# Sigmoid masks of a graph's first tile moved ahead of the last sums, the second tile's spread between evictions, one lookup ahead of the sums, and a normalization ahead of a bit count

## The reference

```python
vals = jnp.where(nd[..., None], x[:, None, :, :], jnp.inf)
s = jnp.sort(vals, axis=2)                  # per node, over its kept neighbours, per channel
nv = nd.sum(2)
for tau, w in zip((0.25, 0.5, 0.75), (0.25, 0.5, 0.25)):
    pos = tau * jnp.maximum(nv - 1, 0)      # lo = floor, hi = ceil, frac
    agg = agg + w * (v_lo + frac * (v_hi - v_lo))
h = jax.nn.relu((x + agg) @ W1 + b1); y = (h @ W2 + b2) * mask
```

## Time and profile before

| | |
|---|---|
| median of 3 runs | 3866.15 us (3860.3 to 3867.21) |
| the profiled execution | 3872.41 us, of which the span is 3870.6 us |
| VectorE busy | 3180.9 us, 82% |
| TensorE matmul busy | 2635.5 us, 68% |
| ScalarE busy | 1949.1 us, 50% |
| one graph in the steady part | 187.7 us |

### The profile page before, as it was taken

One profiled execution on the slowest core, in us unless ns is written; L12 is line 12 of the kernel. 1 busy time (PEld: TensorE's weight loads), 2 busy tenths in 40 slices (PEclk: granted clock), 3 DMA queues, 4 the chain that ended last, 5 costly groups with the idle time before them and its releaser, 6 DMA issues. The chain is left out here.

```text
span 3870.6 us, 48616 instructions
## 1 busy us (share of the span) xinstructions
PE 2635.5 (68%) x16944; PEld 1215.1 (31%) x17098; DVE 3180.9 (82%) x5858; ACT 1949.1 (50%) x2672; POOL 8.0 (0%) x21
## 2 busy tenths in 40 slices
PE   0000155777777877778777778787878787887897
PEld 0000022333333333333333333333323333333665
DVE  8999988888888888787878787878888887855676
ACT  2114444565656565656565646565656565553232
POOL 0000000000000000000000000000000000000000
PEclk6555576898889888888898989888989898887777
DMA  1001001323232323222232323232322222332111
GB/s 36 0 14 46 0 11 22 57 40 56 35 57 37 55 38 56 37 54 39 52 42 50 50 41 57 33 59 35 56 43 48 45 49 44 40 56 39 44 33 33
DMA packets 242849, 158.50 MB, mean 41 GB/s; under 512 B 126504, under 2 KB 228026, under 8 KB 242362
## 3 DMA queue, kind: packets, MB, share of 16 engines
q1 hardware_dynamic: 238490, 154.49, 23.8%
q10 hardware_dynamic: 4128, 1.05, 0.2%
HBM read 40.14 MB, written 14.70 MB: 14 GB/s over the span
## 5 line engine op out<-in xcount | busy, mean ns | idle before, releaser
L1002 ACT ACTIVATE hot<-bcast,consts 128x1024 bf16<-128x1024 f32 x744 | 829.8, 1115 | 487.4 <-PE bcast L567 486.8
L1386 DVE SCALAR_TENSOR_TENSOR prod<-near,consts,rows 128x512 f32<-128x512 bf16 x768 | 566.5, 746 | 323.1 <-PE rows L580 219.5
L580 PE MATMUL rows<-hot,table 128*64 128x512 bf16 x4608 | 729.6, 428 | 115.0 <-DVE prod L1386 103.8
L554 PE MATMUL ring<-member,neigh_t 128*128 128x512 bf16 x1924 | 516.3, 407 | 179.4 <-ACT words L963 149.1
L589 PE MATMUL found_bank<-prod,consts 128*64 128x512 f32 x1536 | 446.3, 656 | 3.9 <-DVE prod L1386 3.9
L567 PE MATMUL bcast<-idx_t,consts 32*128 32x512 f16 x1488 | 315.4, 421 | 171.6 <-ACT hot L1002 158.3
L580 PEld LDWEIGHTS rows<-hot,table 128*64 128x64 bf16 x4608 | 225.9, 116 | 408.8 <-issue 320.4
L554 PEld LDWEIGHTS ring<-member,neigh_t 128*128 128x128 bf16 x2048 | 182.6, 103 | 527.7 <-ACT words L963 193.6
L492 PE MATMUL ring<-identb,adj_b 128*128 128x128 bf16 x256 | 35.6, 272 | 380.1 <-ACT adj_b L890 367.5
L567 PEld LDWEIGHTS bcast<-idx_t,consts 32*128 32x128 f16 x1488 | 71.0, 92 | 540.3 <-ACT hot L1002 364.6
L963 ACT ACTIVATE words<-ring 128x512 uint16<-128x512 f32 x256 | 146.5, 592 | 146.8 <-PE ring L554 146.0
(11 more groups left out here) (332 smaller groups left out, 4371.5 us busy)
## 6 DMA issues: line engine op xcount, KB each, us to landing
near<-idx_bt SPq DMA_DIRECT2D x768, 128.0 KB
late<-in_adj_dram SPq DMA_DIRECT2D x16, 1024.0 KB, 5.6
adjt_d<-late SPq DMA_DIRECT2D x16, 512.0 KB, 2.8
adj_l<-adjt_d SPq DMA_DIRECT2D x16, 512.0 KB, 5.6
adj_s<-adjt_d SPq DMA_DIRECT2D x16, 512.0 KB, 3.5
parts_d<-parts SPq DMA_DIRECT2D x6, 512.0 KB, 5.1
table<-parts_d SPq DMA_DIRECT2D x192, 16.0 KB, 2.2
out_dram<-x_all SPq DMA_DIRECT2D x4, 512.0 KB, 3.8
```

The costliest lines, as they stand in the source:

```text
L554: ins = mm(ring[u % 2][:, :], kept_t[:, j, P * i:P * i + P], member[:, j, n // 2, 512 * (n % 2):512 * (n % 2) + 512], start=(j == 0), stop ...
L580: ins = mm(rows[u % 2][C * h:C * h + C, :], table[:, s, GROUPS * h + g8, :], hot[:, u % HOT, h, :], start=(s == 0), stop=(s == 2))
L1002: run(hot[:, u % HOT].rearrange(flat), spread_bank(l, u)[0][:, 0:2, :].rearrange(flat), ACT.Relu, bias=eq_bias[:, :]).then_inc(S["hot_read ...
L1386: stt(out=prod[:, u % DEEP, :], in0=near[:, u % NEAR, :], scalar=iota_b[:, :], in1=rows[u % 2][:, :], op0=ALU.is_equal, op1=ALU.mult).then ...
```

## The change

Four moves, with nothing added or removed. The three masks of tile 0 go from `select` to the end of the preceding `region`, behind the copies of tile 0's chunks and ahead of `keep_sum` and tile 1's first chunks. Tile 1's three masks go between the copies of its own chunks and the hots, and each hot of `select` stands one place further ahead. TensorE's `units(l, 3)` (spread 4 and lookup 2) goes ahead of chunk 5 and the two sums. VectorE's `pop` (eight instructions) goes behind `gcn_start` and behind unit 30.

```diff
 # TensorE, select
                 chunk(b, 1, 4)
+                units(l, 3)
                 chunk(b, 1, 5)
                 sum_first(b, 0)
                 sum_size(b, 0)
-                units(l, 3)
                 chunk(b, 1, 6)
 # ScalarE, select
                 units(l, 3)
-                for i in range(2):
-                    for k in range(TAUS):
-                        mask(b, i, k)
                 chunk(b, 1, 2)
                 chunk(b, 1, 3)
+                mask(b, 1, 0)
+                units(l, 4)
                 chunk(b, 1, 4)
-                units(l, 4)
+                units(l, 5)
                 chunk(b, 1, 5)
+                mask(b, 1, 1)
                 keep_sums(b, 0)
                 chunk(b, 1, 6)
-                units(l, 5)
+                units(l, 6)
                 chunk(b, 1, 7)
-                units(l, 6)
+                mask(b, 1, 2)
 # ScalarE, region (and the same two lines ahead of the first graph)
                         chunk(p, 0, n)
                         if n == 1:
                             tag(p, 0)
+                    for k in range(TAUS):
+                        mask(p, 0, k)
                 if l is not None:
                     keep_sum(l, d)
 # VectorE, region
                 if p is not None:
                     clear_own(p)
-                if t_of is not None:
-                    pop(wl, x2, x4, x8, t)
                 units(l, STEP[5])
                 if d is not None:
                     gcn_start(d)
+                if t_of is not None:
+                    pop(wl, x2, x4, x8, t)
                 if p is not None:
                     members(p, 1)
```

More of the change, by code:

```diff
@@ L1129, in _ @@
                     tag(0, 0)
+            for k in range(TAUS):
+                mask(0, 0, k)
             for b in range(B):
```

## The result

| | median (range) of 4 runs each | profiled span | clock over the span |
|---|---|---|---|
| before | 3866.68 us (3860.3 to 3867.34) | 3870.6 us | 0.811 |
| after | 3796.47 us (3793.05 to 3804.74) | 3797.5 us | 0.815 |

The ratio is 0.9825 [0.9805, 0.9845]: 70 us faster. I had forecast 107 us and 3759, with a range that ends at 3812. So about a third of the gain is missing.

A forecast was written before the change was run, and what follows sets the result against it. VectorE was taken to bound the kernel, idle 31.6 us per 187.7 us graph, mostly waiting for tile 0's masks. 15 x 5.2 + 14 x 1.9 + 2 = 107 us off 3866 gave 3759, range 3735 to 3812.

The forecast's parts named there:

- Tile 0 (15 x 5.2 + 2 = 80): First tile of a graph: masks made ahead gain 5.2 us in 15 graphs, plus 2 us in the first graph.
- a chunk at the low clock: Tile 1's chunks 2 and 3 ahead of the transposes: one at the low clock makes the delay 3.3 us, not 2.5.
- a steady 1.5: Line 1434 (now 1438), tile 0's size multiply: its 9.15 us wait becomes 1.5, ended by TensorE's transposes.
- my middle: Value 3 of tile 0: 5.2 us gain per graph, taken between 6.2 (all high clock) and 4.3 (low up to lookup 2).
- The 2 us of the first graphs: First graph, with no units beside its tile 0: a smaller wait of the same kind, taken as 2 us.
- the 7.6 of the wait: Shortening of the wait at tile 0's size multiply, forecast to go from 9.15 us to 1.5.
- The `pop` move (14 x 1.9 = 27): In `region`: `x1_ready` 3.6 us earlier lets value 32 follow value 31, gaining 1.9 us in 14 graphs.
- My lower bound: For the `pop` move: 1.2 us per graph, if the low clock holds up lookup 33.
- nothing later eats the lead: Behind tile 0: the lead of about 5 us passes to the next tiles, whose waits keep their size.
- The rival of 0.22: Tile 0: TensorE's clock stays low or `near` loads are late; gain only 30 to 80 us; chance 0.22.
- The slower case: Low clock holds on into tile 1, behind the sums, to 1798: about 94 us slower, 3960; chance 0.05.
- the masks of tile 1: Third mask ends near 1785.4, line 1434 asks at 1789: cover 3.6 us; VectorE waiting for them would refute the forecast.

The follow-up runs named there:

- a1_no_pop: The kernel after with `pop` back ahead of unit 30 and `gcn_start`, so only the other three moves: 3787.03 us, ratio 0.9786 to the kernel before.
- a2_pop_only: The kernel before with only the `pop` move: 3897.75 us, ratio 1.0079 to the kernel before.
- a3_fill: The kernel after with TensorE's first neighbour count, `count_up(p, 0)`, computed five times over: 3776.19 us, ratio 0.9759 to the kernel before.
- c3_pop_fill: The kernel before with the `pop` move and the first neighbour count computed five times over: 3857.04 us, ratio 0.9973 to the kernel before.
- d1_mid_no_pop: The kernel after without the `pop` move and with `middles` ahead of `members(p, 1)`: 3756.71 us, ratio 0.972 to the kernel before.
- a4_middles: The kernel after with VectorE's `middles(p)` ahead of `members(p, 1)` and units 31 and 32: 3770.42 us, ratio 0.9752 to the kernel before.
- c2_tail: The kernel after with chunk 1 of tile 1 computed three times in `region`: 3797.46 us, ratio 0.9816 to the kernel before.
- c1_mid_tail: The kernel after with `middles` early and chunk 1 of tile 1 computed three times: 3753.85 us, ratio 0.9707 to the kernel before.

## Why the prediction was right and where it failed

**Tile 0 (15 x 5.2 + 2 = 80): right, 82 measured.** The main steps are in the trace. The table load stands alone ahead of three masks. The block costs the transposes 2.4 us of delay where I had 2.5: from the end of the last `late` copy to the last transpose it was 9.45 us before (1753.37 to 1762.82) and is 11.86 now (1906.74 to 1918.60). In every second graph it is 4.1 (2089.97 to 2103.52). I had named that case (a chunk at the low clock) and priced it at 3.3 for one chunk; it holds for both. Line 1438 waits 0.75 or 3.16, not a steady 1.5, and value 3's wait is 4.19, in the 4 to 5 forecast. The gain to the start of tile 1, 6.4 or 4.2 us, lies at the bounds of the forecast (6.2 and 4.3), and its mean of 5.3 at my middle. That the number came out so well is partly luck: I had taken the middle as a choice between two cases, and the kernel has both, in turn. In a1_no_pop, which has these three moves alone, the two kinds of graph gain 7.3 and 2.9 us, and graphs 1 to 14 gain 5.2 in the mean.

The Trainium skill ("ScalarE: Activation LUTs", section "What ACT_TABLE_LOAD costs") adds a drain of about 1.38 us to the load. Here again the load takes 1.28 and the first mask starts 1.30 behind its start. The rows and that page differ, as in the kernel before, and the sum was right to go by the row.

**The 2 us of the first graphs: too small.** Graph 1's tile 0 starts its size multiply at 644.2, 12.4 us earlier than at 656.6, where I had 2 and the 7.6 of the wait. By its last such start (3209.6 against 3276.2) the kernel is 66.6 us ahead, and the span is 73 shorter. So the first graphs gave 2.8 us more than the 9.6. Behind the last start the kernel gains another 6.5, where the forecast has a loss of 2.4 (5.2 - 7.6). Together that is near 12 us that I had not forecast and that hid part of what follows: the 14 graphs between gained 54 us where 99 were forecast.

**The `pop` move (14 x 1.9 = 27): wrong in sign.** The step that failed is that value 32 follows value 31 and this is **1.9 us** per graph. Its first half came true to the row. What failed is the silent second half, that nothing behind value 32 moves the other way. I had followed TensorE's queue to lookup 32 and stopped; two entries on stands `count_up(p, 1)` with a release that VectorE sends at a place which had not moved relative to `members`. Its 0.54 us became 3.28. My lower bound named a low clock at lookup 33 and let it eat 0.7 of the 1.9 us; it ate 2.8 to 3.1 (8.54 - 1.82 = 6.7 forecast, 9.54 or 9.79 measured). a2_pop_only shows the cost by itself, and a3_fill and c3_pop_fill show that the clock behind the gap is its cause, since they change nothing but what TensorE does in the gap. The time lies in the stated range even so, but not because this term was right: the range was made wide for a loss in tile 0, and the 12 us at the two ends helped.

The Trainium skill ("TensorE: Matmul & The Clock Gate", Part 1) has the clock fall after idleness. I used it for tile 0, where it decided little, and not here, where a release was left behind and so an idle time was made. The rows agree with the page here: 0.96 mean from 1888 to 1897 before, 0.61 behind the gap after, 1.00 with the gap filled. At the masks' gap they agree in part: behind the same 2.32 us the chunks had the low clock in every second graph of the kernel after and in no steady graph of d1_mid_no_pop.

**Even mended, the move gives 12 us or less.** The other half of the error is the sentence that nothing later eats the lead. It was said of tile 0's lead, and I let it stand for this one too. In c3_pop_fill the 1.9 us are there at value 34 and gone by the next graph's value 31, 1.1 of them at value 2; its later graphs take what they took before. Graphs 12 to 14 of the kernel before had shown this ahead of any run. And with `middles` early value 32 does not wait even where `x1_ready` comes late (d1_mid_no_pop), so the wait that the move was to remove is no longer there. That d1_mid_no_pop beats a4_middles by 14 us goes back to three long graphs in the latter. Whether the move brings these about is not settled: the runs of a4_middles spread over 14 us, and only one of each kernel is profiled.

**The rivals.** The rival of 0.22, part of the gain lost to a clock that stays low, is what happened in kind, though at a place that I had not named; it was set at tile 0, where it is in every second graph. The slower case did not come: from the sums on TensorE has its full clock. Nor did the masks of tile 1 hold VectorE.

**Left open.** Why graphs come in pairs of two lengths in the kernel after and a1_no_pop, and are all alike in d1_mid_no_pop and c2_tail, is seen and not explained. TensorE's gap behind the masks is 2.32 us in both halves, and the chunks behind it are slow in one only. What the pairing costs is not shown either. The two lengths differ by 1.1 us in the kernel after and by 4.4 in a1_no_pop, and c2_tail ends the pairing but brings a low clock behind line 1438 in its place.

## What to carry to other kernels

When a signal is moved earlier, follow the receiving engine's queue past the instruction that it frees, to the next wait that the same sender releases: that wait can grow by most of what the first one lost, unless its sender is moved too (here 0.54 to 3.28 us, when the first wait shrank by 3.55). Price a new gap on TensorE with the clock behind it: here 3.3 us of idleness cost 2.9 us up to value 34, of which 2.0 were left a graph later, and computing the same product five times in it was faster than leaving it idle. Follow a lead through a whole graph before it is multiplied by the number of graphs. And test a mend without the move that made it needed: `middles` early was worth some 26 to 30 us on the kernel without the `pop` move, and with the move on top the kernel was no faster.

## What the runs showed of the hardware

- Work that nobody needs can shorten a kernel: 16 repeated matmuls per graph in the gap took 20 us off the kernel after and 41 off a2_pop_only. Eight at the other gap took nothing off the kernel after (c2_tail) and 16 us off a4_middles (c1_mid_tail).
- A TensorE gap of the same 2.32 us, behind the same instructions, was followed by the full clock in one graph (8 matmuls in 1.90 us, 1.00 granted) and by a lower one in the next (3.51 us, 0.52 granted). In a1_no_pop, with 1.90 and 3.39 us, graphs take 180.4 and 184.8 us in turn over whole stretches; in d1_mid_no_pop the gap is the same and every steady graph has the 1.90.
- A Sigmoid table load between copies, 1.28 us, is followed by the first activation 1.29 or 1.30 us behind its start, in 14 graphs each of all 14 kernels.
